# A fused attention and fp8 layer on one core: the first queries of group 1 travel through a buffer of their own

## The reference

```
x = x + attention(layernorm(x))
x = x + ffn(layernorm(x))
```

## Time and profile before

| | us |
|---|---|
| runs | 538.99, 540.0, 542.82 |
| median | 540.0 |
| profiled execution | 537.49 |
| its span | 535.6 |
| TensorE busy | 491.2 (92%) |
| ScalarE busy | 487.1 (91%) |
| VectorE busy | 279.4 (52%) |
| GpSimd busy | 218.1 (41%) |

### The profile page before, as it was taken

One profiled execution on the slowest core, in us unless ns is written; L12 is line 12 of the kernel. 1 busy time (PEld: TensorE's weight loads), 2 busy tenths in 40 slices (PEclk: granted clock), 3 DMA queues, 4 the chain that ended last, 5 costly groups with the idle time before them and its releaser, 6 DMA issues.

```text
span 535.6 us, 9389 instructions
## 1 busy us (share of the span) xinstructions
PE 491.2 (92%) x3457; PEld 113.3 (21%) x3457; DVE 279.4 (52%) x652; ACT 487.1 (91%) x528; POOL 218.1 (41%) x281
## 2 busy tenths in 40 slices
PE   8767999999999999999999999999999999999951
PEld 3311211231121211231121212222111212121210
DVE  5523454454744555554754554554555655455546
ACT  2756999999999999999999999999999999999941
POOL 0789406974251218993251217994101211002110
PEclk9998999999999999999999999999999999999995
DMA  5368979746997101757977100747987000100000
GB/s 174 121 229 210 278 220 242 274 143 201 261 206 182 48 5 33 278 170 213 256 164 161 26 5 7 276 170 223 259 181 165 22 5 7 47 0 1 1 21 24
DMA packets 48707, 73.79 MB, mean 138 GB/s; under 512 B 6096, under 2 KB 26512, under 8 KB 48528
## 3 DMA queue, kind: packets, MB, share of 16 engines
q1 hardware_dynamic: 47840, 72.85, 49.3%
q10 hardware_dynamic: 816, 0.28, 0.2%
HBM read 35.40 MB, written 35.65 MB: 133 GB/s over the span
## 4 chain that ended last, share of the span: by engine, by line
PE 47%; ACT 32%; issue 9%; DVE 5%; DMA 3%; POOL 2%; SPq 1%; DVEq 0%; POOLq 0%; ACTq 0%
ACT probs L730 32%; PE ps L926 25%; PE ps L910 14%; PE ps L828 1%; PE ps L795 1%; PE ps L823 1%; PE ps L791 1%; DVE ps L1150 1%; PE ps L800 1%; DMA qp_dram<-parts 1%; DMA Qs<-qp_dram 1%; DMA X<-L_attn_x 1%; PE ps L835 0%; POOL parts L589 0%; POOL sq L587 0%
## 5 line engine op out<-in xcount | busy, mean ns | idle before, releaser
L730 ACT ACTIVATE probs<-ps 128x1024 f32<-128x1024 f32 x512 | 479.8, 1065 | 17.3 <-DVE ps L1150 11.6
L926 PE MATMUL ps<-probs,V 128*9 128x512 f32 x2048 | 268.6, 596 | 3.9 <-DVE pv_out L1158 1.2
L1150 DVE TENSOR_TENSOR ps<-ps,consts 128x256 f32<-128x256 f32 (+1 forms) x256 | 144.4, 566 | 182.6 <-PE ps L910 175.9
L910 PE MATMUL ps<-Qs,Ks 64*128 64x512 bf16 x992 | 181.8, 386 | 18.1 <-ACT probs L730 5.1
L910 PEld LDWEIGHTS ps<-Qs,Ks 64*128 64x128 bf16 x992 | 43.8, 93 | 289.5 <-ACT probs L730 267.7
L926 PEld LDWEIGHTS ps<-probs,V 128*9 128x9 f32 x2048 | 31.3, 88 | 79.3 <-issue 58.3
L626 POOL TENSOR_TENSOR xs<-xs,magic 128x512 f32<-128x512 f32 x7 | 8.9, 1277 | 92.4 <-DVE magic L1211 92.4
L543 POOL TENSOR_SCALAR rs<-mv 128x4 f32<-128x4 f32 (+1 forms) x10 | 2.3, 228 | 82.7 <-DVEq L1332 82.0
L565 POOL TENSOR_TENSOR sq<-kT,decay 128x256 f32<-128x256 f32 (+2 forms) x13 | 16.2, 1249 | 47.8 <-DVE kT L1250 33.4
L1158 DVE COPY pv_out<-ps 105x512 f32<-105x512 f32 x31 | 21.4, 692 | 25.8 <-PE ps L926 25.8
L577 POOL TENSOR_TENSOR sq<-sq,parts 128x1024 f32<-128x1024 f32 (+1 forms) x16 | 29.3, 1834 | 1.3
(11 more groups left out here) (142 smaller groups left out, 285.7 us busy)
## 6 DMA issues: line engine op xcount, KB each, us to landing
Qs<-qp_dram SPq DMA_DIRECT2D x26, 512.0 KB, 9.5
qp_dram<-parts SPq DMA_DIRECT2D x16, 768.0 KB, 4.7
Ks<-kp_dram SPq DMA_DIRECT2D x26, 384.0 KB, 5.9
kp_dram<-parts SPq DMA_DIRECT2D x12, 384.0 KB, 3.8
kp_dram<-parts SPq DMA_DIRECT2D x6, 768.0 KB, 5.0
qp_dram<-parts SPq DMA_DIRECT2D x8, 512.0 KB, 6.0
Qs<-qp_dram SPq DMA_DIRECT2D x12, 256.0 KB, 8.5
X<-L_attn_x SPq DMA_DIRECT2D x10, 256.0 KB, 3.0
```

The costliest lines, as they stand in the source:

```text
L730: nc.scalar.activation(probs[:, quad % RING, 2 * jp:2 * jp + 2, :].rearrange("p j n -> p (j n)"), ps_all[:, bank * CH:(bank + 2) * CH], AC ...
L910: last = nc.tensor.matmul(bank, Ks[half, g, jp, key_cols(v, kc)], Qs[half, g, jp, qh, v, :], start=True, stop=True)
L926: last = nc.tensor.matmul(pv[32 * j:32 * j + VW, :], V[:, unit // 2 * NB + kc, HG * j + g, :], probs[:, quad % RING, j, :], start=i == 0, ...
L1150: nc.vector.tensor_tensor(own, own, factors, ALU.mult).then_inc(fixed, 1)
```

## The change

Group 1's first queries no longer go through `qp_dram`. A new buffer `fq_dram` of 32 rows by 8 products by 1024 (bfloat16, 512 KB) takes them: eight stores, two for each of the four heads (products 0 to 5, written as two copies of three parts; products 6 and 7), each reading eight partitions. Two loads bring them to `Qs[:, 1]`. The order in SyncE's queue changes: the first key loads are issued as soon as the early keys 0 are stored, then the eight stores, a wait for them, the query loads, the stores of early keys 1, and only then the 2 MB of early queries, which groups 2 and 3 still read. The wait for these comes after the second key loads.

```
+            def store_first_queries(g):
+                sp.wait_ge(parts_ready, pieces_made(0, "early queries"))
+                for rows in FIRST_ROWS:
+                    n = rows.stop - rows.start
+                    times, taken = max(1, n // PARTS), min(n, PARTS)
+                    for j in range(HG):
+                        own = slice(32 * j + HD * g, 32 * j + HD * g + HD)
+                        sp.dma_start(fq_dram[HD * j:HD * j + HD, rows, :].rearrange("p (a r) n -> p a (r n)", a=times),
+                                     parts[own, 1, 0:taken, :].rearrange("p (o r) n -> p o (r n)", o=1)
+                                     .broadcast_to([HD, times, taken * S])).then_inc(first_out, 16)
+
+            def load_first_queries(g):
+                sp.wait_ge(first_out, 16 * len(FIRST_ROWS) * HG)
+                for i in range(2):
+                    q_rows = fq_dram.rearrange("(t p) r n -> p r t n", t=2)[HD * i:HD * i + HD, :, :, :]
+                    sp.dma_start(Qs[64 * i:64 * i + 64, g, :, 0, :, :].rearrange("p t v n -> p t (v n)"),
+                                 q_rows.rearrange("d r t n -> (d r) t n")).then_inc(stage_in[g], 16)
...
             store_keys(0, "early keys 0", early_keys[0], 0)
-            store_queries(0, "early queries", 0)
             sp.wait_ge(parts_out[0], 16 * STORED)
-            sp.wait_ge(parts_out[1], 16 * STORED)
             load_keys(0, 1, early_keys[0], stage_in[1])
-            load_queries(0, 1, slice(0, 1), stage_in[1])
+            store_first_queries(1)
+            load_first_queries(1)
             store_keys(0, "early keys 1", early_keys[1], KL)
+            store_queries(0, "early queries", 0)
             sp.wait_ge(parts_out[0], 16 * STORED * 2)
             load_keys(0, 1, early_keys[1], stage_more)
+            sp.wait_ge(parts_out[1], 16 * STORED)
             for g in range(2, G):
                 load_keys(0, g, early, stage_in[g])
                 load_queries(0, g, slice(0, 1), stage_in[g])
```

More of the change, by code:

```diff
@@ L41 @@
 STORED = 3
+FIRST_ROWS = slice(0, 2 * PARTS), slice(2 * PARTS, PRODUCTS)
 KL = S // 2
@@ L144, in build @@
 def build(nc, x, wq, wkT, wvT, wo, wd, wuk, wuv, w8, s_in, s_k, bias, decay_rows, decay_table,
-          const_cols, out, qt_dram, kt_dram, qp_dram, kp_dram):
+          const_cols, out, qt_dram, kt_dram, qp_dram, kp_dram, fq_dram):
     with ExitStack() as ctx:
@@ L261, in build @@
         stage_more = sem("stage_more")
+        first_out = sem("first_out")
         stage_late = [sem(f"stage_late{g}") for g in range(G)]
@@ L442, in _ @@
             store_keys(0, "early keys 0", early_keys[0], 0)
-            store_queries(0, "early queries", 0)
-            sp.wait_ge(parts_out[0], 16 * STORED)
-            sp.wait_ge(parts_out[1], 16 * STORED)
-            load_keys(0, 1, early_keys[0], stage_in[1])
-            load_queries(0, 1, slice(0, 1), stage_in[1])
-            store_keys(0, "early keys 1", early_keys[1], KL)
+            sp.wait_ge(parts_out[0], 16 * STORED)
+            load_keys(0, 1, early_keys[0], stage_in[1])
+            store_first_queries(1)
+            load_first_queries(1)
+            store_keys(0, "early keys 1", early_keys[1], KL)
+            store_queries(0, "early queries", 0)
             sp.wait_ge(parts_out[0], 16 * STORED * 2)
             load_keys(0, 1, early_keys[1], stage_more)
+            sp.wait_ge(parts_out[1], 16 * STORED)
             for g in range(2, G):
@@ L1518 @@
     kp_dram = nc.dram_tensor("kp_dram", (B, P, PRODUCTS, KN), BF16, kind="Internal").ap()
-    build(nc, *args, out, qt_dram, kt_dram, qp_dram, kp_dram)
+    fq_dram = nc.dram_tensor("fq_dram", (HG * HD, PRODUCTS, S), BF16, kind="Internal").ap()
+    build(nc, *args, out, qt_dram, kt_dram, qp_dram, kp_dram, fq_dram)
     r = run_bass_kernel_spmd(nc, [arrays], core_ids=[0])
```

## The result

| | runs | median, us | lowest to highest |
|---|---|---|---|
| before | 17 | 539.52 | 537.44 to 542.82 |
| after | 17 | 544.18 | 541.77 to 545.89 |

The ratio is 1.0082, with a 95% interval of 1.0066 to 1.0098: **slower by 4.4 us** (0.0082 x 539.5), where 2.5 us less was forecast. It is above the range (541.0), though within the 1% that was called no change. The profiled execution took 545.43 us with a span of 543.6, beside 537.49 and 535.6.

The account below looks back on a forecast made before the run. ScalarE's exponentials bound the long stretch, so only the earlier stall at quad 8 could shrink. Gains of 2.6 + 1.4 us, cut to 2.5 by quad 32, took the 540.0 median to 537.5 us, range 534.5 to 541.0.

Parts of the forecast that it names:

- Step 1: Group 1's keys: both key loads issued by 26.5 us, before the queries are ready, at no cost.
- Step 2: Eight small query stores: 0.63 us of issue each, 5.35 us for eight with gaps, landed at 34.2 us.
- rival B: Small stores dear at 1.2 us each and the queue's lateness decides: slower by about 2.1 us, 542.1; chance 0.13.
- Step 3: Group 1's query loads: issued at 34.2 and 34.8 us, so quad 8 starts at 38.6, 2.6 us earlier.
- Step 4: TensorE's clock around quad 8: no fall after the shorter stand, another 1.4 us gained before ScalarE's steady stretch.
- Step 5: Query stores and second key loads moved back: a new wait of 1.0 us at quad 12, mostly hidden.
- Step 6: SyncE's queue behind the start: 1.4 us later, against 3.9 us of slack at quad 32; 2.5 us gain passes.
- T2: Theory formed after the result: the order costs, 2 MB of stores behind the second key stores, whatever the small stores take.
- The sum: Whole kernel: 2.6 + 1.4 us gained, less what quad 32 doesn't let through, leaving 2.5 us faster.
- A: Small stores cheap at 0.36 us each: quad 8 at 36.6 us, quad 32 lets 4.6 through, 535.4; chance 0.2.
- C: The wait only moves: query loads land at 40.8 us or second keys near 50; no change, 539.5 to 540; chance 0.17.

Follow-up runs that it names:

- e1: Reordering alone against the kernel after: early key loads kept, queries through the old three 128-partition stores, no small stores; 537.31 us, ratio 0.9967.
- e2: The kernel after with the same eight small stores in head order 0, 2, 1, 3; 541.54 us, ratio 1.0032.
- e9: The kernel before, in its order, with the eight small stores added behind group 1's second key loads, their output never loaded; 547.30 us, ratio 1.0153.
- e3: The kernel after with each small store reading 32 partitions of a quarter of the width, changing group 1's query values; 541.10 us, ratio 1.0035.
- e7: The kernel before, unchanged, run again for a second trace; 540.0 us.
- e8: The kernel after again, unchanged, for a second trace; 543.74 us.
- e4: The kernel after with group 3's gather in batch 0 issued ahead of batch 1's early key stores; 543.9 us, ratio 1.0071.
- e13: The kernel after with batch 2's X load and batch 1's early key stores issued after group 3's last gather; 544.57 us, ratio 1.0088.
- e15: e1 with batch 2's X load and batch 1's early key stores issued after group 3's last gather; 538.14 us, ratio 0.9971.
- e12: e1 with the 512 KB load of batch 2's input issued two groups later; 538.60 us, ratio 0.9989.

## Why the prediction was wrong

*Step 1, the keys early: right.* They were issued at 25.29 and cost nothing (e1).

*Step 2, the eight stores: the mis-sized term.* Between 0.36 and 1.36 us a store, 0.63 was taken by the nearest row in shape, a gather of 16 KB. A store of 96 KB from eight partitions isn't near it. It measured 0.97 us on average, with 1.40 to 1.77 where a store had to wait. The sum so was 7.76 us for 5.35, and the landing was seen at 37.05 and not at 34.2. The prediction reckoned 190 GB/s for these stores from the number of DMA engines; the rows show 49. The number of engines alone is not what bound: e2 left the shapes as they were and gained 1.9 us by sequence. The Trainium skill has a rule for it that the prediction passed over, in "SBUF — State Buffer", section "Door 1: The DMA port swizzle (why `[64,N]` ≈ `[32,N]`)": the bandwidth goes by how many of 16 ports the partitions reach, four neighbouring partitions and those 32 above them share one. Eight partitions are two ports, an estimate of 54 GB/s by that page's rate, and the stores for j = 0 and 1 share theirs. This case's 49 GB/s and e2's gain agree; the times of single stores (0.28 us in e9 for one that shares the ports of the store ahead, 1.14 in e2 for one that doesn't) don't follow from it. By the rule 512 KB through two ports at a time are 9.7 us, an estimate of 1.2 us a store, and rival B, which decides from 0.95, would have been the forecast.

*Step 3, the query loads: right where its input was.* From 34.65 they land for a quad 8 at 39.24 in e3 (38.6 forecast from 34.2). In after the input was 2.9 us late, and the 2.6 us of gain became 0.3 of loss.

*Step 4, the clock: right in e3, wrong as a rule.* After a stand of 1.41 us the clock stayed at its full level, 2.4 GHz. After 2.81 us in e2 it did not. The columns of the earlier trace rows:

```profile
39.00:40.00 1.00, 0.89 (x6) 0.22 (x10) 0.43 (x1) 0.00 (x0) 0.68 (x4) 0.83 1.09 385
40.00:41.00 1.00, 1.00 (x8) 0.00 (x0) 0.00 (x0) 0.93 (x1) 0.72 (x4) 0.50 1.08 380
```

The step reasoned that in before the clock still read full from 40 to 41 us, 3.4 us into the stand. It left out that the clock can fall once TensorE is at work again: in e2 it was full to the end of the stand and read 0.50 behind it. So each new stand of 2.5 us at quad 32 or 39 cost more than its length: 4.3 us between e7 and e8 for a stand of 2.3 on ScalarE.

*Step 5, the second keys at quad 12: right,* 1.43 us in e3 beside 1.0, and 0.43 us in after again, where quad 8 came late.

*Step 6, the queue behind: the step that failed, and the sign with it.* It set 1.4 us of lateness against 3.9 us of slack at quad 32, so that 2.5 us of gain would pass. e3 measures it with step 2 held right. The lateness came out about right: the loads for quad 32 were issued at 79.13, 2.3 us behind 76.82, and about 0.9 of that is the late beginning of this whole execution, TensorE's too.

Two things were wrong. First the slack: the 7.9 us of the earlier trace rows are a median over a pair of loads from each one's issue, and I counted them from the first issue. In the trace of before the second load, issued at about 77.45, landed 8.8 us on, at 86.3. The slack was 2.9. Second, a term that the step didn't have: a fetch of instructions, 16 KB in 1.3 us, at the moment at which the loads end. In e3 it ran from 87.30 to 88.65; of the 256 packets of 4 KB of these two loads 255 had ended by 87.6, and the last ended at 89.07. It is the same in e2 and e4, about 1.4 us each. It isn't chance that they meet: in every trace this fetch begins within about 0.6 us of TensorE's arrival at quad 32 (88.63 in before, where the data had ended at 85.46), so it lies in the way of just those loads that are late. 1.4 + 1.4 leaves 0.1 of the 2.9, and nothing of quad 8's gain passes quad 32.

In absolute times 86.3 + 2.3 + 1.4 = 90.0, where e3 has its 90.02. In after, whose data ended at 90.51 with the fetch from 90.91 on, the sum is 91.5 without the fetch (measured 91.50, and the stand came at quad 39), and in after again, 0.9 later and with it, 93.8 (measured 93.74). And the step looked at one consumer only: the gather of group 3 has 2 MB of stores ahead of it, and VectorE waits for it in order, so that it holds up the exponentials. So T2 keeps a part: in e3 it is the 2 MB moved back that make the queue late, 1.4 us as reckoned (e1, which doesn't move them back, issues the loads for quad 32 at 77.01), and dear stores make it later.

*The sum.* The forecast is a ratio of 0.9954 (2.5 of 540.0), e3 1.0035, after 1.0082. So about 2.5 us of the miss (0.47%) are step 2, and about 4.4 us (0.81%) are step 6 with the clock's part in it; the intervals make the first uncertain by about 1.5 us and the second by 1.3.

*The rivals.* B named the mechanism, one of the two places and nearly the time, 542.1, and had a chance of 0.13. The chance was too low for a reason that stood in the text: its price of a store was inside the bounds, and the forecast's rested on a row of another size. A fell with step 2; whether stores of 0.36 us would have gained anything wasn't run, and at 0.63 (e3) nothing was gained. C saw the wait at quad 12 and not the one that counted.

*Left open.* How often the lateness meets quad 32 and how often quad 39 isn't known, with two traces of after. In after again the data ended at 91.42, the fetch ran from 91.23 to 92.49, and TensorE started 2.3 us behind the data, where it is otherwise about 1.0. In e13 the fetch (from 89.52) began before the data's end (89.87) as well, and nothing was late; the traces don't say which DMA engine carried what, so that the fetch is the cause is read from the times alone. Why single stores wait as they do is open. That GpSimd's waits are what makes unit 3's gather late in e13 is read from one trace and was not tested.

## What to carry to other kernels

Price a transfer by the partitions that it reads as well as by its bytes, and try narrow stores in another sequence (here 5.9 us for 7.8). When something is put into an in-order queue, list every later consumer of that queue, gathers too, with the last landing of each in the trace, and take the smallest slack: the gain ends there, and a stand adds a slow clock to its length. Moving what is in the way of one consumer puts it in the way of the next; of the 13 variants here, only two (e1 and e15) were faster than before, by 0.3%, and both have no small stores and the key loads moved forward into idle time; a third of this kind, e12, wasn't clear of no change.

## What was not expected of the hardware

- Eight small stores of 512 KB in all take 7.76 us of issue, and 5.90 in another sequence. Behind them in a full queue three 128-partition stores take 3.80 us of issue, where they take 2.07 otherwise.
- Where an instruction fetch of 16 KB (1.3 us) fell on the end of a load on which TensorE waited, the last packet came 1.4 us late, in three traces.
- VectorE's product at L1192 takes 1.57 us in after at 109.74, and 0.69 in before, with GpSimd at work beside it; a step on 128 numbers takes 1.86 us for 0.15 in e9.
